# Half a token chunk of the feed-forward part, moved into the last attention step

## The reference

```python
qkv = einsum('bsd,ed->bse', x, w_qkv) + b_qkv
scores = q @ k.T / sqrt(32) + causal          # causal mask, per head
out = softmax(scores) @ v                     # heads joined
x = layernorm(x + out @ w_out.T + b_out)
hidden = relu((x @ sign(up_weight).T) * up_scale)
y = (hidden @ sign(down_weight).T) * down_scale * output_scale
x = layernorm(x + y)
```

## Time and profile before

| | |
|---|---|
| median of three runs | 775.22 us |
| the profiled execution: its own time | 774.34 us |
| its span in the trace | 772.6 us |
| TensorE busy | 722.7 us, 94% |
| VectorE busy | 450.5 us, 58% |
| ScalarE busy | 317.2 us, 41% |
| GpSimd busy | 354.4 us, 46% |
| last attention step's scores in `ps_proj`, a bank that only this step's scores use | start from 429.4 to 478.7 us |
| its last block of narrow matmuls ends | 483.1 us |

### The profile page before, as it was taken

How to read it: one execution, slowest core, us unless ns; L and a number is a source line. 1 busy time by engine, 2 the same in 40 slices (tenths; PEclk the granted TensorE clock), 3 DMA queues, 4 the chain that set the end, 5 groups by cost and what they waited for, 6 DMA issues and landing times.

```text
span 772.6 us, 11683 instructions
## 1 busy us (share of the span) xinstructions
PE 722.7 (94%) x4032; PEld 505.2 (65%) x4032; DVE 450.5 (58%) x1086; ACT 317.2 (41%) x631; POOL 354.4 (46%) x487
## 2 busy tenths in 40 slices
PE   6899999999999999999979889999999999999993
PEld 4788665655656556565544544788778787878882
DVE  4176495785967859678567751633294339334515
ACT  5211365654655546555546565432232222122210
POOL 4461467394673946739423502632353235223333
PEclk9999999999999999999999999999999999999998
DMA  6976464435544355452677331313012001000101
GB/s 231 296 208 177 110 174 124 136 105 163 150 132 132 108 157 148 115 133 88 174 206 261 109 123 58 120 32 119 14 41 95 28 1 41 15 1 12 44 1 54
DMA packets 44619, 85.71 MB, mean 111 GB/s; under 512 B 4880, under 2 KB 13584, under 8 KB 44432
## 3 DMA queue, kind: packets, MB, share of 16 engines
q1 hardware_dynamic: 35536, 79.72, 34.2%
q10 hardware_dynamic: 9024, 5.24, 2.4%
HBM read 55.33 MB, written 29.36 MB: 110 GB/s over the span
## 4 chain that ended last, share of the span: by engine, by line
PE 71%; DVE 19%; issue 3%; DMA 3%; POOL 2%; ACT 2%; SPq 0%; ACTq 0%; POOLq 0%
PE ps_heads L1045 9%; PE ps_proj L1087 7%; DVE heads_sb L835 7%; PE ps_proj L947 7%; PE ps_score L1104 6%; PE ps_unit L1063 6%; PE ps_unit L1087 5%; PE ps_sum L1039 5%; DVE maxes L813 5%; PE ps_unit L983 4%; PE ps_heads L1104 3%; PE ps_unit L1015 3%; PE ps_sum L1104 3%; PE ps_score L1015 2%; PE ps_score L983 2%
## 5 line engine op out<-in xcount | busy, mean ns | idle before, releaser
L655 POOL TENSOR_TENSOR hid_low<-hid_raw,hid_high 128x512 fp32r<-128x512 f32 x64 | 85.1, 1330 | 175.0 <-DVE hid_high L886 171.9
L711 ACT ACTIVATE probs<-ps_unit 128x512 f32<-128x512 f32 (+3 forms) x216 | 101.9, 490 | 88.4 <-PE ps_unit L1015 85.0
L619 POOL TENSOR_SCALAR_AFFINE_SELECT probs<-probs 128x128 f32<-128x128 f32 x256 | 73.1, 298 | 113.0 <-ACT probs L711 108.9
L711 ACT ACTIVATE probs<-ps_score 128x512 f32<-128x512 f32 (+3 forms) x155 | 75.2, 498 | 77.0 <-PE ps_score L1015 75.6
L886 DVE CAST hid_high<-hid_raw 128x512 fp32r<-128x512 f32 x64 | 27.1, 424 | 125.4 <-ACT hid_raw L766 125.2
L809 DVE CUSTOM_DVE_ANT_0 ps_unit<-ps_unit,causal 128x512 f32<-128x512 f32 (+3 forms) x162 | 80.1, 511 | 32.5 <-PE ps_unit L983 31.5
L1045 PE MATMUL ps_heads<-probs,v_rows 128*32 128x512 f32 (+3 forms) x768 | 80.3, 502 | 11.8 <-DVE heads_sb L837 11.8
L983 PE MATMUL ps_unit<-stack 96*128 96x512 f32 (+3 forms) x246 | 83.8, 354 | 5.7 <-DVE maxes L809 2.5
L1015 PE MATMUL ps_unit<-stack 98*128 98x512 f32 (+2 forms) x216 | 78.4, 366 | 4.1 <-DVE maxes L809 4.0
L613 POOL TENSOR_TENSOR parts<-qk_full,parts 128x512 fp32r<-128x512 f32 x32 | 41.3, 1289 | 64.7 <-ACT parts L690 64.4
L835 DVE RECIPROCAL heads_sb<-ps_sum 128x128 f32<-128x128 f32 x64 | 60.8, 950 | 9.2 <-PE ps_sum L1039 9.2
(11 more groups left out here) (195 smaller groups left out, 1478.0 us busy)
## 6 DMA issues: line engine op xcount, KB each, us to landing
stack<-qk_parts SPq DMA_DIRECT2D x96, 256.0 KB, 4.6
qk_parts<-parts SPq DMA_DIRECT2D x32, 512.0 KB, 2.9
v_all<-h_even ACTq DMA_DIRECT2D x16, 256.0 KB, 3.8
v_rows<-v_all SPq DMA_DIRECT2D x8, 512.0 KB, 4.3
heads_t<-heads_sb SPq DMA_DIRECT2D x16, 256.0 KB, 3.4
raw<-up_w SPq DMA_DIRECT2D x8, 512.0 KB, 3.9
x_tile<-x_rows SPq DMA_DIRECT2D x16, 256.0 KB, 5.5
raw<-down_w SPq DMA_DIRECT2D x8, 512.0 KB, 3.4
```

What stands on the lines that cost most here:

```text
L655: nc.gpsimd.tensor_tensor(hid[1][:, (HM * s + n) % 3, :], hid_raw[:, n % 2, :], hid[0][:, (HM * s + n) % 3, :].bitcast(FP32), ALU.subtract ...
L711: nc.scalar.activation(probs[:, (NP * s + n) % RING, 0:width], bank(what, s, n)[:, off:off + width], ACT.Exp, scale=SCALE).then_inc(s_exp, 1)
```

## The change

The feed-forward part now runs in five rounds in place of four chunks: `ROUNDS` has tiles 0 and 1 of chunk 0 as round 0, tiles 2 and 3 as round 1, and then the three other chunks whole. A round of two tiles has `up` matmuls of 256 columns in place of 512, and two `down` tiles in place of four; it does its 16 + 16 steps with half the work in each.

- Round 0 stands in step 7: `up` at `last` + 14 + 2.05 m, `down` at `last` + 18.4 + 2.05 m. Its hidden rows have buffers of their own (`hid0`), and its sums go to `ps_unit[0]` and `ps_unit[1]`.
- Round 1 starts at `FIRST_UP`. All of chunk 1's `split` to `turn` now stand beside it, in 16 slots of half the work. `attn` of chunk 1 writes `ps_unit[0]`, so it waits for round 0's `z`.
- `attn` of chunk 0 moves forward: tile 0 to `late` + 44.5, tile 1 to `late` + 47.1, tiles 2 and 3 to `last` + 2.5 and 5.5. `norm1` and `turn` move from `last` + 23 and on to `last` + 9 and on.
- The scores of step 7 lose `ps_proj` and, from piece 15 on, `ps_unit[2]`: three banks in turn, then two.
- The groups of step 7 stand in pairs (13, 13, 19.6, 19.6, ...), six blocks of two groups where there were twelve of one. The divisions of both last steps move.
- The weight jobs are ordered by use, and the last of them is due at `last` + 36 where six stood behind `FIRST_UP`.

```diff
-         [10, 12.4, 15, 17.5, 24, 28, 31.5, 35, 38.5, 42.5, 46, 48.6]]
-ALONE_NORM = [[18.4, 18.41, 18.42, 18.43, 50.4, 50.41, 50.42, 50.43],
-              [17.6, 17.61, 17.62, 17.63, 48.7, 48.71, 48.72, 48.73]]
+         PAIRED[:10] + [49, 49]]
+ALONE_NORM = [[19.25, 19.26, 19.27, 19.28, 50.4, 50.41, 50.42, 50.43],
+              [19.7, 19.71, 19.72, 19.73, 49.05, 49.06, 49.07, 49.08]]
...
+ROUNDS = [(0, (0, 1)), (0, (2, 3))] + [(i, tuple(range(TT))) for i in range(1, CH)]
+TILES = [0, 2, 4, 8, 12, 16]
+FILL_FROM = 15
+
+JOBS = [("out", 0), ("out", 1)] + [("up", k) for k in range(4)] + [("down", 0), ("down", 1), ("up", 4), ("down", 2), ("up", 5),
+        ("down", 3), ("up", 6), ("down", 4), ("up", 7), ("down", 5), ("down", 6), ("down", 7)]
...
-    signs = [late + 23, late + 25.5] + [late + 29 + 4.6 * k for k in range(4)] + [late + 50.2 + 4.5 * k for k in range(4)]
-    signs += [late + 88, late + 92] + [FIRST_UP + 1, FIRST_UP + 3] + [FIRST_UP + 7 + 2 * k for k in range(4)]
+    last = NP * (STEPS - 1)
+    signs = [late + 23, late + 25.5] + [late + 28.5 + 3.6 * k for k in range(4)] + [late + 43, late + 46]
+    signs += [last + at for at in (3, 6, 9.5, 13, 16.5, 20, 24, 28, 32, 36)]
...
-    for i in range(4):
-        put(late + 38 + 2 * i, "split", 0, i)
-        put(late + 46.5 + 1.3 * i, "bias", 0, i)
+    for i in range(TT):
+        put(late + 37.5 + 1.5 * i, "split", 0, i)
+        put(late + 40 + 1.3 * i, "bias", 0, i)
         for m in range(12):
-            put(last + 0.5 + 5.2 * i + 0.42 * m, "attn", 0, 12 * i + m)
-        put(last + 5.8 + 5.2 * i, "y", 0, i)
-        put(last + 23 + i, "norm1", 0, i)
-        put(last + 26 + 2.5 * i, "turn", 0, i)
-    put(last + 22.5, "std1", 0)
+            put((late + 44.5, late + 47.1, last + 2.5, last + 5.5)[i] + 0.22 * m, "attn", 0, 12 * i + m)
+        put((late + 47, last + 2.2, last + 7.7, last + 8.2)[i], "y", 0, i)
+        put(last + 9 + 0.1 * i, "norm1", 0, i)
+        put((last + 10.2, last + 10.9, last + 12.6, last + 13.2)[i], "turn", 0, i)
+    put(last + 8.6, "std1", 0)
+    for r, (i, tiles) in enumerate(ROUNDS):
+        t = FIRST_UP + 16 * (r - 1)
         for m in range(HM):
-            put(t + m, "up", i, m)
-            if i < CH - 1 or m < HM - 2:
-                put(t + m + 2.5, "down", i, m)
+            put(t + m if r else last + 14 + 2.05 * m, "up", r, m)
+            if r < len(ROUNDS) - 1 or m < HM - 2:
+                put(t + m + 2.5 if r else last + 18.4 + 2.05 * m, "down", r, m)
...
+        end = t + 17.55 if r else FIRST_UP + 2.1
+        for q in tiles:
+            put(end, "z", i, q)
+            put(end + 1.05 + q, "ln2", i, q)
+            put(end + 1.95 + q, "out", i, q)
...
             for q in range(TT):
-                put(t + 2.2 + 0.7 * q, "split", i + 1, q)
-                put(t + 3 + q, "bias", i + 1, q)
+                at = 2 * q if i else 2.5 * q
+                put(t + (2.2 + 0.7 * q if i else 0.3 + 0.4 * q), "split", i + 1, q)
+                put(t + (3 + q if i else 1 + q), "bias", i + 1, q)
                 for m in range(12):
-                    put(t + 5.2 + 2 * q, "attn", i + 1, 12 * q + m)
-                put(t + 6 + 2 * q, "y", i + 1, q)
-                put(t + 6.7 + 2 * q, "ln1", i + 1, q)
-                put(t + 7.4 + 2 * q, "turn", i + 1, q)
+                    put(t + (5.2 if i else 3) + at, "attn", i + 1, 12 * q + m)
+                put(t + (6 if i else 4.3) + at, "y", i + 1, q)
+                put(t + (6.7 if i else 5.1) + at, "ln1", i + 1, q)
+                put(t + (7.4 if i else 6.3) + at, "turn", i + 1, q)
...
-    order, had, users = [3, 4, 5, 0, 1, 2], {}, {}
+    order, had, users = [3, 4, 0, 1, 2], {}, {}
...
-            may = (2, 3, 4, 5) if s == STEPS - 1 else (0, 1, 2, 3, 4)
+            may = (2, 3, 4)[n >= FILL_FROM:] if s == STEPS - 1 else (0, 1, 2, 3, 4)
...
+        def down_bank(r, i):
+
+            return ps_unit[i] if r == 0 else ps_down[i - 2] if r == 1 else ps_down[i]
...
                     if m == 0:
-
-                        wait(pe, s_y, TT * s + i - (s == 0))
...
+                        if s == 1:
+
+                            pe.wait_ge(s_z, 1)
...
+                    if s == 0 and n == 0:
+
+                        dve.wait_ge(s_pv, NP * STEPS)
                     dve.wait_ge(s_dt, TT * s + n + 1)
```

More of the change, by code:

```diff
@@ L387, in build @@
         up_b = sb(late, "up_b", [P, HM // 2, DC, P], FP32R)
+        hid0 = [sb(late, f"hid0_{n}", [P, 3, 2 * P], FP32R) for n in ("high", "low")]
+        hid0_raw = sb(late, "hid0_raw", [P, 2, 2 * P], FP32)
         t_odd = [sb(late, f"t_odd_{n}", [P, DC, HALF], FP32R) for n in ("high", "low")]
@@ L431, in bank @@
         def bank(what, s, n):
-            return (ps_unit + ps_score + [ps_proj])[users[what, s, n][0]]
+            return (ps_unit + ps_score)[users[what, s, n][0]]
         def hidden_used(eng, steps):
@@ L439, in hidden_used @@
             elif steps > 0:
[L440 removed]
+                eng.wait_ge(s_dt, TILES[steps // HM])
         def x_piece(b, n):
@@ L1056, in _ @@
                             pe.wait_ge(s_wol, 2)
[L1057 to L1063 removed]
+                            pe.wait_ge(s_qk, NB * STEPS)
+                        if s == 1:
+                            pe.wait_ge(s_z, 1)
+                    if s == 0 and m == 0 and i > 1:
+                        bank_read(last_user[i - 2])
+                    if m == 0 and (s > 0 or i == 1):
+                        wait(pe, s_y, TT * s + i)
+                    mm = nc.tensor.matmul(attn_bank(s, i)[:, :], turned[s % 2][xp][:, c, i * P:(i + 1) * P], wo[wp][:, c, :],
                                           start=(m == 0), stop=(m == 11))
@@ L1068, in _ @@
                     pe.wait_ge(s_h1, TT * s + n + 1)
-                    wait(pe, s_tl, TT * s + n)
+                    if s > 0 or n == 3:
+                        pe.wait_ge(s_tl, TT * s + n if s else 2)
+                    if s == 1 and n == 0:
+                        pe.wait_ge(s_z, 2)
                     for c in range(DC):
-                        mm = nc.tensor.transpose(ps_turn2[:, c * P:(c + 1) * P], h1[s % 2][:, n, c * P:(c + 1) * P],
+                        mm = nc.tensor.transpose(turn_bank(s, n)[:, c * P:(c + 1) * P], h1[s % 2][:, n, c * P:(c + 1) * P],
                                                  ident[:, :])
@@ L1091, in _ @@
                 if what == "down":
+                    i, tiles = ROUNDS[s]
                     if s == 0:
-                        pe.wait_ge(s_sign, 11 + n // 2)
+                        pe.wait_ge(s_sign, JOBS.index(("down", n // 2)) + 1)
                     pe.wait_ge(s_hdl, HM * s + n + 1)
-                    if s == 0 and n == 0:
-                        pe.wait_ge(s_exp, NP * STEPS)
-                    for i in range(TT):
-                        if s == 0 and n == 0 and i == 2:
+                    for q in tiles:
+                        if n == 0 and s == 0:
+                            pe.wait_ge(s_tl, 4)
+                        if n == 0 and s == 1:
+                            pe.wait_ge(s_exp, NP * STEPS)
+                        if n == 0 and s == 2:
+                            pe.wait_ge(s_z, min(3 + q, 4))
@@ L1099, in _ @@
                             pe.wait_ge(s_norm, QT * STEPS)
-                        if n == 0:
-                            wait(pe, s_z, TT * (s - 1) + i + 1)
+                        if n == 0 and s > 2:
+                            pe.wait_ge(s_z, TT * (i - 1) + q + 1)
                         for part in range(2):
-                            mm = nc.tensor.matmul(ps_down[i][:, :], hid[part][:, (HM * s + n) % 3, i * P:(i + 1) * P],
-                                                  down_sb[:, down_at(n), :], start=(n == 0 and part == 0),
+                            at = (q - tiles[0]) * P
+                            mm = nc.tensor.matmul(down_bank(s, q)[:, :], hidden(s)[0][part][:, (HM * s + n) % 3, at:at + P],
+                                                  down_sb[:, n, :], start=(n == 0 and part == 0),
@@ L1114, in _ @@
                     for m in (HM - 2, HM - 1):
-                        pe.wait_ge(s_hdl, HM * s + m + 1)
+                        pe.wait_ge(s_hdl, HM * r + m + 1)
                         for part in range(2):
-                            mm = nc.tensor.matmul(ps_down[n][:, :], hid[part][:, (HM * s + m) % 3, n * P:(n + 1) * P],
-                                                  down_sb[:, down_at(m), :], start=False, stop=(m == HM - 1 and part == 1))
+                            mm = nc.tensor.matmul(ps_down[n][:, :], hid[part][:, (HM * r + m) % 3, n * P:(n + 1) * P],
+                                                  down_sb[:, m, :], start=False, stop=(m == HM - 1 and part == 1))
```

116 lines of the change are left out of this document (59 added, 57 removed).

## The result

| | before | after |
|---|---|---|
| median, us (runs) | 775.42 (4) | 789.71 (4) |
| from, to | 774.33, 776.11 | 788.33, 790.59 |
| ratio after/before | | 1.0184 [1.0163, 1.0205] |
| profiled execution, span | 774.34, 772.6 | 789.04, 787.2 |
| granted clock, mean | 0.991 | 0.976 |

A forecast was written before the change was run, and what follows sets the result against it. TensorE, busy 94% of the span, was taken as the bound, with gains only from idle, low clock or switching. Terms -0.5 + 2.2 + 1.0 - 1.0 + 7.1 = +8.8 us on 775.22 gave 784.0; range 774 to 792.

The forecast's parts named there:

- Part 1: Division of step 6 moved from 18.4 to 19.25: earlier score banks, later division; -0.5 us, between -1.0 and 0.
- Part 2: End of step 6: early fourth up sign holds the exps, attn of tile 1 waits for y; +2.2 us, 0 to +4.
- Part 3: Start of step 7: TensorE waits 5.1 us for VectorE's chain to the first transpose; +1.0 us, -1 to +3.
- Part 4: Middle of step 7: half-width matmuls cost 0.9, pairing saves 2.4, score banks and division cost 0.5; -1.0 us.
- term for pairing: Step 7: six narrow blocks fewer, at 0.42 us of switching each, save 2.4 us (0 to 2.5).
- Part 5: Step 7 into round 1: TensorE waits 5.3 us for z, then low clock and another wait; +7.1 us, +2 to +10.
- second wait: Round 1: attn of the second tile waits for y of the first, behind z, ln2 and out; about 1.0 us.
- forecast's own case: Whole kernel: the terms hold as summed, 780 to 788 us; chance 0.50.
- The two score banks: Step 7: every second of 31 scores waits 0.25 us for its exp, 4 us dearer, 788; chance 0.20.
- smaller case: Steps 6 to round 1: transfer lands early, clock stays up, splits are short; +3, 778 us; chance 0.12.
- faster rival: Step 7 and round 1: the filling works, no long idle or low clock is left; -6.8, 768.4 us; chance 0.12.

The follow-up runs named there:

- first experiment: Changed kernel with the sign of the fourth up job back at late + 42.8, the next two at + 45.2 and + 48.5: 786.21 us, 1.0136.
- third experiment: Changed kernel with the first pair of narrow blocks of step 7 at slot 10.1, ahead of the first transpose, in place of 13: 789.33 us, 1.0176.
- mended kernels: Changed kernel with sign back, last divisions behind z, first pair ahead and four more edits: 772.35 us; with step 6's last projection later as well: 771.58.
- the three edits: Changed kernel with sign back, last divisions behind z and first blocks ahead of the transpose, all together: 778.63 us, 1.0045.
- second experiment: Changed kernel with the four last divisions spread behind z, at last + 54.1 to 61.6 in place of 49.05: 786.57 us, 1.0143.

## Why the prediction was right, and where its size was off

What the prediction named as its signs is there: 4.54 us before the first transpose, released by the norm; 5.70 before chunk 1's first `attn`; ScalarE's 3.68 for the transfer; granted clocks of 0.69 and 0.66 behind the two idles; half steps of 0.96 us; no repeated waits for exps in the middle.

- **Part 1** (-0.5 us; 0 to -1.0). The block of 401.15 is at 402.12, 0.97 late where the trace was 1.37 late before it, so 0.4 gained. But the low clock behind lasts on (0.52 in 404 to 408), and the next block, at 406.28 before, starts at 408.50: the lag has grown to 2.22, so +0.85 for the part.
- **Part 2** (+2.2). ScalarE's 3.68 us (over 3 forecast) and TensorE's 3.40 (3.2) are as worked out, 1.17 for 0.8. Two things were missed: the wait for the maxima did not vanish (1.26), and the part had no low clock in it, though the block behind takes 1.51 + 1.51 us. The first experiment shows that this second miss is not the sign's: it stayed without the 3.40.
- **Part 3** (+1.0). 4.54 us, released by the norm; forecast 5.1. The third experiment shows that it is the chain of the norm and not the pair's place: with the pair moved ahead 1.39 + 1.90 us remained, and the time.
- **Part 4** (-1.0). The middle has no waits for exps, as forecast. A half step is 0.96 us (475.09 to 476.05; 0.94 forecast). The term for pairing (2.4) is not borne out: the ledgers of the two kernels with pairs alone leave 0.9 and 1.3 us for it; yet the whole remainder of the ledger here is -3.2 for the -1.5 that part 4 held beside waits and clock (0.9 - 2.4), so some 2 us of gain aren't placed.
- **Part 5** (+7.1). 5.70 us against 5.3, but in part by errors that cancel. The divisions started 0.74 us behind the last narrow block (0.2 in the sum), as a split of 1.14 stood in front of them; the three splits took 0.68, 0.69 and 1.21 where 1.78 was taken for the third; and the second cast took 1.35 for 0.25. By the rule of the Trainium skill ("SBUF — State Buffer", section "SBUF: two separate sides") the three splits could all have met GpSimd's subtraction, for 7.4 (7.5 by the sum's own terms). The trace agrees for one of the three, the one of 1.21, beside a subtraction that GpSimd began at 523.25; the wait lies between the two ends. Its second wait failed: 2.60 us before the second tile's `attn` where 1.0 stood, since a late hidden cast is in front of `y`.
- **The term that was mis-sized** is the low clock. Idles were forecast at +8.8 net and are +10.6. The low clock was priced where an idle was over 5 us (parts 3 and 5), at 1.5 us each, with the 1.5 of before taken off: +1.5. It came to +5.8: 2.3 of it stand near 430, where the forecast had none, and 1.0 and 0.9 more near 404 and 460 than before. Between the spans the forecast is short by 5.8 us: 4.3 of low clock, 1.8 of idle and 1.4 of the late start, less 1.7 of the remainder.
- **The range.** Its ends don't follow from the terms that it names. Parts 2 and 5 at their low ends give 776.7 (774 was written), part 4 at its upper end gives 788.5 (792 was written). The measured 789.71 lies above the second and above the forecast's own case of 780 to 788, so that the range held it is partly luck.
- **Rivals.** The two score banks (788 by its sum) is nearest by time and wrong by cause: no repeated waits for exps. The smaller case adds up to +4.0 by its own terms, not +3; it did not happen either way. The faster rival needed that no long idle be left; the mended kernels are that case, and came to 772.35 and 771.58, not 768.4.

Open: what lowers the clock near 430 (behind 3.40 + 1.26 us and behind 0.95 + 1.33, not behind before's 1.00 + 0.82), what pairing saves free of side effects (0.9 to 1.3 us by the ledger of two kernels), whether the three edits add to more than their sum, and what holds the `up_weight` transfer for 8.6 us.

## What to carry to other kernels

When work is moved to fill a matmul engine, list for each of the other engines what now stands in front of the next instruction that TensorE waits for: here an early sign, four divisions, the splits and the order of `z`, `ln2`, `out` and one transpose. Seven edits to such places turned 1.8% slower into 0.4% faster. Expect low clock with new idle time (here +5.8 us for +10.6 of idle), but don't count on getting it back with one idle: a wait of 3.40 us went, and the low clock stayed. Undo or mend the waits together before judging the idea: three of the edits alone gave 0.6 to 3.7 us, all seven 17.6. And compare the result with the best kernel without the idea, not only with the one you started from.

## What was not expected of the hardware

- Behind idles of 3 to 6 us the granted clock was 0.52 to 0.69 of full over one or two of the 4 us rows above; +10.6 us of idle came with +5.8 us of loss at 1.2 GHz. The length of the idle does not decide alone. The 2.60 us had no low clock behind them (1.00 from 536 on), while the 2.49 in the second experiment and the same `y` wait in the third (2.59) did; and 0.95 + 1.33 us had it in the first, where before's 1.00 + 0.82 had none. The second, then the third:

```profile
524.00:528.00 4.00, 3.10 (x7) 2.46 (x8) 3.48 (x7) 0.00 (x0) 3.77 (x4) 0.62 0.01 2
```

```profile
536.00:540.00 4.00, 2.38 (x6) 1.90 (x7) 3.79 (x11) 0.59 (x2) 0.73 (x1) 0.68 0.19 70
```

- A VectorE cast of 128x256 with a single SBUF input took 1.35 us in one case, 0.72 in another and 0.29 in most; during the long one this GpSimd addition ran:

```profile
524.32 1.71 POOL L682 TENSOR_TENSOR x_tile<-x_tile,b_out_sb 128x512 f32<-128x512 f32 x1
```

- The same first 85 us of the program ended at 85.10 to 86.97 in ten traces: a profiled span alone can't settle 2 us.
